# Moving the low half of the next head's rotated query from VectorE to GpSimd in an attention and FFN kernel

## The reference

```python
DIM_Q, H, K, D_C, D_CQ, R = (512, 16, 128, 128, 384, 64)
q_hk = (hidden_q @ Wq.T).reshape(Bv, Sv, H, K)
q_big = jnp.einsum('bshk,hkq->bshq', q_hk, w_kc_q)
q_big = _apply_rope(q_big, sin_q[None, :, None, :], cos_q[None, :, None, :])
kv_r = _apply_rope(kv_c, sin_k[None], cos_k[None])
q_r = jnp.einsum('bshq,hqr->bhsr', q_big, W_qr)
k_r = jnp.einsum('bld,hdr->bhlr', kv_r, W_kr)
scores = jnp.einsum('bhsr,bhlr->bhsl', q_r, k_r)
attn = jax.nn.softmax(scores, axis=-1)
ctx_c = jnp.einsum('bhsl,bld->bhsd', attn, kv_r)
ctx_lat = jnp.einsum('bhsd,hkd->bhsk', ctx_c, w_kc_kv)
ctx = ctx_lat.transpose(0, 2, 1, 3).reshape(Bv, Sv, H * K)
return ctx @ Wo.T
```

## Time and profile before

| | before |
|---|---|
| median of 3 runs | 858.98 us (858.0 to 860.82) |
| span of the profiled execution | 861.5 us |
| PE busy | 757.3 us, 88% |
| DVE busy | 766.2 us, 89% |
| ACT busy | 573.6 us, 67% |
| POOL busy | 577.6 us, 67% |
| mean granted TensorE clock | 0.966 |
| chain that ended last | PE 35%, POOL 20%, DVE 18%, issue 11%, DMA 7%, SPq 5%, ACT 3% |

### The profile page before, as it was taken

One profiled execution on the slowest core, in us unless ns is written; L12 is line 12 of the kernel. 1 busy time (PEld: TensorE's weight loads), 2 busy tenths in 40 slices (PEclk: granted clock), 3 DMA queues, 4 the chain that ended last, 5 costly groups with the idle time before them and its releaser, 6 DMA issues.

```text
span 861.5 us, 12578 instructions
## 1 busy us (share of the span) xinstructions
PE 757.3 (88%) x3268; PEld 487.1 (57%) x3268; DVE 766.2 (89%) x1026; ACT 573.6 (67%) x838; POOL 577.6 (67%) x581
## 2 busy tenths in 40 slices
PE   3678998989999999999999999999999675868996
PEld 3555565756666666666566656665666442424543
DVE  5799899989998999899989999999999767797895
ACT  2477677767766867687667766776777576774332
POOL 5769674867486757766776668576848474867462
PEclk9889999999999999999999999999999797889999
DMA  9216867776768576858676766677668999400000
GB/s 330 79 49 115 169 130 140 138 167 134 151 114 170 117 161 132 170 111 167 118 160 134 152 128 138 149 137 150 125 146 213 241 227 275 164 0 25 13 24 37
DMA packets 294405, 118.50 MB, mean 138 GB/s; under 512 B 271856, under 2 KB 278000, under 8 KB 294128
## 3 DMA queue, kind: packets, MB, share of 16 engines
q1 hardware_dynamic: 293568, 116.68, 62.0%
q10 hardware_dynamic: 816, 1.57, 0.5%
HBM read 49.02 MB, written 2.10 MB: 59 GB/s over the span
## 4 chain that ended last, share of the span: by engine, by line
PE 35%; POOL 20%; DVE 18%; issue 11%; DMA 7%; SPq 5%; ACT 3%; POOLq 1%; DVEq 0%; ACTq 0%
PE banks L1419 22%; POOL rot_cos L1055 5%; PE scores L1720 5%; DMA load<-in_pack 4%; POOL rot_lo L1063 4%; SPq L943 4%; PE scores L1507 3%; PE banks L1735 3%; DVE neg_max L1323 3%; POOL rot_hi L1061 2%; DVE rows L1330 2%; POOL rot_sin L1046 2%; DVE rot_cos L1295 2%; DVE cv_lo L1288 1%; POOL wq_lo L388 1%
## 5 line engine op out<-in xcount | busy, mean ns | idle before, releaser
L1185 ACT ACTIVATE scores<-scores,neg_max 128x1024 f32<-128x1024 f32 x128 | 139.2, 1087 | 56.1 <-DVE neg_max L1323 54.6
L1330 DVE SCALAR_TENSOR_TENSOR rows<-scores,rows 128x1024 f16<-128x1024 f32 x128 | 154.9, 1220 | 13.7 <-ACT rows L1196 12.6
L1419 PE MATMUL banks<-pt,v_hi 128*128 128x512 f16 x512 | 154.3, 383 | 12.5 <-DMA pt<-rows 11.4
L1323 DVE TENSOR_REDUCE neg_max<-scores 128x1 f32<-128x1024 f32 x128 | 155.5, 1216 | 2.9 <-PE scores L1507 2.7
L1055 POOL TENSOR_TENSOR rot_cos<-rot_cos,rot_sin 128x512 f32<-128x512 f32 x93 | 119.2, 1281 | 46.6 <-DVE rot_sin L1297 42.2
L1196 ACT ACTIVATE rows<-scores 128x1024 f16<-128x1024 f32 x128 | 130.8, 1022 | 5.2
L1063 POOL TENSOR_TENSOR rot_lo<-rot_cos,rot_hi 128x512 fp32r<-128x512 f32 x93 | 119.6, 1286 | 7.8
L1159 ACT CAST cv_hi<-banks 128x512 fp32r<-128x512 f32 x64 | 37.6, 587 | 102.6 <-PE banks L1419 101.4
L1318 DVE SCALAR_TENSOR_TENSOR acc<-banks,inv,acc 128x512 f32<-128x512 f32 x128 | 91.4, 745 | 8.0 <-PE banks L1419 4.1
L1419 PE MATMUL banks<-pt,v_lo 128*128 128x512 f16 x256 | 97.8, 382 | 0.0
L1419 PEld LDWEIGHTS banks<-pt,v_hi 128*128 128x128 f16 x512 | 44.5, 98 | 79.2 <-issue 36.4
(11 more groups left out here) (211 smaller groups left out, 1824.7 us busy)
## 6 DMA issues: line engine op xcount, KB each, us to landing
load<-in_pack SPq DMA_DIRECT2D x15, 320.0 KB, 3.5
raw_chunk<-in_out_w SPq DMA_DIRECT2D x8, 512.0 KB, 5.2
raw_chunk<-in_gate_w SPq DMA_DIRECT2D x8, 512.0 KB, 4.4
raw_chunk<-in_val_w SPq DMA_DIRECT2D x8, 512.0 KB, 4.6
raw<-in_gate_w SPq DMA_DIRECT2D x8, 512.0 KB, 5.5
raw<-in_val_w SPq DMA_DIRECT2D x8, 512.0 KB, 5.2
raw<-in_out_w SPq DMA_DIRECT2D x8, 512.0 KB, 7.0
load<-in_pack SPq DMA_DIRECT2D x15, 256.0 KB, 3.3
```

The lines of the kernel that those rows point to most:

```text
L1185: nc.scalar.activation(scores[:, u % 2, :], scores[:, u % 2, :], ACT.Exp, bias=neg_max[:, u:u + 1], accum_out=sums[:, u:u + 1]).then_inc(e ...
L1323: nc.vector.tensor_reduce(neg_max[:, u:u + 1], scores[:, u % 2, :], AX, ALU.max, negate=True).then_inc(max_ready, 1)
L1330: nc.vector.scalar_tensor_tensor(out=rows[:, u % ROWS, 1, :], in0=scores[:, u % 2, :], scalar=WEIGHT_LIFT, in1=rows[:, u % ROWS, 0, :], op ...
L1419: mm = nc.tensor.matmul(out, ws[a], xs[c], start=first and n == 0, stop=last and n == 2)
```

## The change

For the queries of heads 1 to 15 (C0 and C1 with "next"):

- ACT copies the whole bank (128 rows, fp32) to `rest`, and rows 0 to 63 to qr_hi rows 0 to 63. This is all that is read from the bank, and PE's wait for it is on ACT's count `group_hi`.
- POOL, from the entries C0 and C1 of its order, writes `upper_rest` (rest rows 0 to 63 less qr_hi), a tile in the place of qr_hi rows 64 to 127, waits for it, and writes qr_lo rows 64 to 127 (rest rows 64 to 127 plus upper_rest). It counts `query_low` and waits for that itself.
- ACT's doubling waits for `query_low`, and copies both qr_hi and qr_lo, so it is two instructions in place of one.
- DVE's two instructions and the entries C0 and C1 in its orders are gone.

The opening's own query, head 0's, stays as it was. The core of the diff:

```diff
 EVEN_POOL = (
-    ("w", 2), ("rot", 0, 0), ("rot", 0, 1), ("rot", 0, 2), ("w", 3), ("rot", 1, 0), ("rot", 1, 1), ("rot", 1, 2),
-    ("w", 0), ("w", 1),
+    ("w", 2), ("rot", 0, 0), ("rot", 0, 1), ("rot", 0, 2), ("w", 3), ("rot", 1, 0), ("rot", 1, 1), C0, ("rot", 1, 2),
+    ("w", 0), C1, ("w", 1),
 )
...
+    def bank_copied(self, group):
+
+        g, earlier = self.bank_last_used(group)
+        if g is None or not by_pool(g):
+            return None
+        if earlier:
+            return self.start_hi + self.before_highs.index(g) + 1 - len(self.before_highs)
+        return self.hi(g)
...
+        upper_rest = nc.alloc_sbuf_tensor_at("upper_rest", [P, B, S], F32, offset=at["qr_hi"])
...
+            def query_rest(p, marked):
+
+                b, low = marked[1], slice(R, 2 * R)
+                n = p.head.plus(1).after(B, b + 1 - B)
...
+                pool.wait_ge(group_hi, p.hi(marked))
+                if p.head.i is not None:
+                    apart()
+                nc.gpsimd.tensor_tensor(upper_rest[low, b, :], rest[0:R, b, :], qr[0][0:R, b, :].bitcast(F32),
+                                        ALU.subtract).then_inc(query_rested, 1)
+                pool.wait_ge(query_rested, n)
+                if p.head.i is not None:
+                    apart()
+                nc.gpsimd.tensor_tensor(qr[1][low, b, :], rest[low, b, :], upper_rest[low, b, :], ALU.add).then_inc(query_low, 1)
+                pool.wait_ge(query_low, n)
...
+                elif by_pool(marked):
+                    nc.scalar.copy(rest[:, group[1], :], src)
+                    out, src = qr[0][0:R, group[1], :], banks[0:R, p.bank[marked], :]
...
             def double(p, marked):
 
                 b = marked[1]
-                done = p.earlier(("C", b, "next")) if marked[-1] == "last" else p.place(("C", *marked[1:]))
-                act.wait_ge(group_read, p.read(done))
+                if p.first and len(marked) == 2:
+                    act.wait_ge(group_read, p.emptied_at(("C", b)))
+                else:
+                    h = p.head if marked[-1] == "last" else p.head.plus(1)
+                    act.wait_ge(query_low, h.after(B, b + 1 - B))
+                    nc.scalar.copy(qr[0][R:2 * R, b, :], qr[0][0:R, b, :])
                 nc.scalar.copy(qr[1][0:R, b, :], qr[1][R:2 * R, b, :]).then_inc(doubled, 1)
...
+                if not k and p.bank_copied(marked) is not None:
+                    pe.wait_ge(group_hi, p.bank_copied(marked))
```

More of the change, by code:

```diff
@@ L123 @@
     ("O", 1, 2, "last"), ("low", 3), ("O", 1, 3, "last"), A1, ("max", 4), ("M",), ("B", 1, 0, "next"),
-    ("B", 1, 1, "next"), ("max", 5), C0, ("low", 4), ("low", 5), ("K", 0, 0, "next"), ("K", 0, 1, "next"),
+    ("B", 1, 1, "next"), ("max", 5), ("low", 4), ("low", 5), ("K", 0, 0, "next"), ("K", 0, 1, "next"),
     ("B", 1, 2, "next"), V0, ("max", 6), ("O", 0, 0), ("max", 7), ("O", 0, 1), ("low", 6), ("O", 0, 2), ("O", 0, 3),
-    C1,
 )
@@ L271, in sine_by_pool, with by_pool @@
     return group[0] == "B" and group[-1] == "next" and group[1:3] in SIN_BY_POOL
+def by_pool(group):
+    return group[0] == "C" and group[-1] == "next"
 def two_engines(group):
@@ L319, in __init__ @@
             self.before = [(g, BANK[1 - odd][g]) for g in BEGUN[1 - odd]]
-            self.before_full, self.before_emptied = ALL[1 - odd], EMPTIED[1 - odd]
+            self.before_full, self.before_emptied, self.before_highs = ALL[1 - odd], EMPTIED[1 - odd], HIGHS[1 - odd]
             self.start = head.after(GROUPS, GROUPS_BEFORE)
             self.start_hi = head.after(HI_GROUPS, HI_BEFORE)
+            self.start_empty = head.after(EMPTIES, EMPTIES_BEFORE)
     def full(self, group):
@@ L329, in emptied_at @@
     def emptied_at(self, group):
-        return self.start + self.place(group)
+        return self.start_empty + self.place(group)
     def read(self, *places):
-        return self.start + max(places)
+        return self.start_empty + max(places)
     def place(self, group):
@@ L343, in hi, with bank_last_used @@
         return self.start_hi + self.highs.index(group) + 1
-    def bank_free(self, group):
+    def bank_last_used(self, group):
         bank = self.bank[group]
@@ L349, in bank_free @@
             if self.bank[g] == bank:
-                return self.place(g)
+                return g, False
         for g, used in reversed(self.before):
             if used == bank:
-                return self.before_emptied.index(g) + 1 - len(self.before_emptied)
-        return None
+                return g, True
+        return None, False
+    def bank_free(self, group):
+        g, earlier = self.bank_last_used(group)
+        if g is None or by_pool(g):
+            return None
+        return self.earlier(g) if earlier else self.place(g)
+    def bank_copied(self, group):
+        g, earlier = self.bank_last_used(group)
+        if g is None or not by_pool(g):
+            return None
+        if earlier:
+            return self.start_hi + self.before_highs.index(g) + 1 - len(self.before_highs)
+        return self.hi(g)
     def earlier(self, group):
@@ L1106, in period @@
                 for item in POOL_ORDERS[p.head.number % 2]:
-                    if item[0] == "rot":
+                    if by_pool(item):
+                        query_rest(p, item)
+                    elif item[0] == "rot":
                         b = item[1]
```

25 lines of the change are left out of this document (16 added, 9 removed).

## The result

| | before | after |
|---|---|---|
| median | 858.49 us (856.54 to 860.82, 4 runs) | 920.18 us (920.01 to 925.02, 4 runs) |
| span of the profiled execution | 861.5 us | 918.1 us |
| mean granted TensorE clock | 0.966 | 0.939 |
| DVE busy | 766.2 us | 723.7 us |
| POOL busy | 577.6 us | 654.5 us |

The changed kernel takes 1.0707 times as long (95% interval 1.0674 to 1.074): 61.7 us more by the medians. The forecast was 914 us, and its text gives 905 to 922 for its own spread and reaches down to 890 for the rivals.

The account below looks back on a forecast made before the run. At the end of even periods PE waits for POOL, which was taken to have no slack there. 7 x (6.1 + 1.1) + 5 = 55.4 on the profiled 861.5, against the median 914 us; own spread 905 to 922, reaching to 890.

Parts of the forecast that it names:

- ACT's doubling waiting for POOL with V0 queued behind it: End of even periods: doubling moves to 338.15, O products start at 340.8 instead of 335.80, PE idle for 5.0.
- +6.1: Even period: wc is split until 353.1 and PE starts B at 353.2 instead of 347.15.
- half time on POOL: Rival: POOL's instructions on half the partitions take 0.64, odd periods hide all; 884 us, chance 0.07.
- The clock holds: Rival: PE's 5.0 of idleness brings no half rate, B starts at 351.95, +4.8 per even period; 903 us, chance 0.14.
- faster: Rival: DVE is the bound and POOL's extra work is slack, 2.3 off each pair; 843 us, chance 0.04.
- Nothing on this stretch has slack: End of even periods: POOL's rotations, wq's split, wc's load and split, and PE's start behind them leave no spare time.
- rot_lo ends 1.1 later, and PE waits 1.1 longer: Odd periods: POOL's C0 lasts 2.8, of which 1.75 was idle, so PE's existing wait at 382.24 grows by 1.1.
- a second idle stretch: Part of the case slower than all others, beside C1 being late for more; chance 0.05.
- 7.2: Loss per pair of periods: 6.1 in the even kind plus 1.1 in the odd kind, counted seven times.
- The opening: Opening period, ending like an even one: wc is split some 5 later than it was, +5.
- The 2.3: Even periods: loss from 12 matmuls at half rate after PE's 5.0 idle, making C1 full at 347.3 instead of 345.0.
- 350.2: Even periods: time when wc's load, behind tile 6's transposes on SP, would be in.

Follow-up runs that it names:

- e1: Changed kernel with ACT's doubling of C0 moved behind V0 and tile 6's exponential and high part in even and opening periods; 900.83 us, ratio 1.0469.
- e2: Changed kernel with C0's low part placed ahead of rotations (1,0) and (1,1) in POOL's order, ACT's order unchanged; 897.24 us, ratio 1.0421.
- e5: Changed kernel with C0 put back on DVE, so only C1's low part is made by POOL; 858.88 us, ratio 0.998.
- e6: Changed kernel with C1 put back on DVE, so only C0's low part is made by POOL; 927.55 us, ratio 1.0772.
- e7: Changed kernel with both groups' low instructions on DVE from SBUF, none on POOL, ACT's copies and doublings kept; 866.21 us, ratio 1.0074.
- e4: e3 plus 8 thrown-away products on PE ahead of C1's third part in odd periods; 910.53 us, ratio 1.0575.
- e3: Changed kernel with 20 thrown-away products on PE ahead of the first O group in even periods and the opening; 914.98 us, ratio 1.0627.
- e9: e2 with 15 thrown-away products on PE ahead of C1's first part in even periods and the opening; 883.96 us, ratio 1.0266.

## Why the prediction was right, and where it was off

**Right: the place and the chain of waits.** The forecast rested on ACT's doubling waiting for POOL with V0 queued behind it. It said that ACT would double from 338.15 and the O products start at 340.8 after 5.0 of PE's idle time; they stand at 338.33 and 340.83, after 4.97. B in the even period was put at 353.2 and came at 353.28: +6.1, as said. And C1's end: ACT was to begin its copies at 347.3, POOL to end at 351.3; they did at 347.38 and 351.30. e1 and e2 show that the wait is a real cost and not only a visible one (1.8 and 1.5 of the even period), e5 and e6 that C0 alone carries it.

**Right: the time of a POOL instruction on 64 partitions.** 1.28 was assumed and 1.26 to 1.30 measured, so the rival "half time on POOL" (884) falls. "The clock holds" (903) falls by the rows after 365.89, "faster" (843) by ACT's 4.99 of waiting, since it needed POOL to be ready before ACT; and e5 shows, for C1's half, that even where POOL takes the work at no cost the time that DVE saves moves nothing. One sentence went too far: "Nothing on this stretch has slack". POOL's pause before wc's load held C1 (e5) and 0.57 us of longer rotations (e7) without a later B.

**Off: the odd period.** The step "rot_lo ends 1.1 later, and PE waits 1.1 longer" was right for the wait (1.2: C1's third part follows B after 36.30, before after 35.09), but I stopped there. The idle stretch of 2.00 that this makes is followed by the level of 1.2 GHz as well, in six of the seven odd periods, and costs 1.7 (B after 8.94 for 7.20; 1.6 by e4, whose 7.36 leaves 0.16 that is not the clock's). I had asked what the clock does after the gap of 5.0 and not after the one of 2.0, though the earlier trace rows has gaps of 3.05 and 4.30 only and so said nothing of 2.0; "a second idle stretch" stood only in the last case, at 0.05. So a pair is 6.1 + 1.2 + 1.7 = 9.0, not 7.2; the trace has 8.9.

**Off by little.** The opening costs 4.4, not 5. The seventh pair with the last period costs 5.2, less than the others: its odd period has no fall to half rate (idle stretch 1.63), and the head after its even period has no successor, so there is no wc to split at its end. Sum: 4.4 + 6 x 8.9 + 5.2 = 63 up to the first `hidden` of the FFN, which starts at 808.96, before at 745.88. The two spans then differ by only 56.6, since the FFN was 6.5 shorter in this execution. The medians, 61.7 apart, show that little of that is kept in most runs. So it is luck that the profiled span, 918.1, lies only 1.2 above the sum (861.5 + 55.4): the odd periods were priced too low, and the FFN's stretch, which is no part of the argument, gave most of it back.

**Right where it fell, smaller where it counts: the clock in the even period.** The 2.3 was right for the O products and C1: C1's first product starts 5.15 after the first O (371.04 less 365.89), before 2.80. Of that, 1.3 was to reach B; by e3 it is 0.9 at best, because wc's load, which I had put at 350.2, came at 350.7: without the fall B comes at 352.5 and not at 351.95. The prediction had 6.1 with the fall and 4.8 without; it is 6.1 and 5.3.

**What makes a pair's 8.9.** Even kind, 5.9: POOL's delay of the rotations 2.8 (e9), the clock 0.7 (e3), and by difference 2.4 for ACT's wait with V0 behind it. Odd kind, 3.0: the clock 1.6 (e4), POOL's delay 1.2, and 0.2 not taken apart. This is an estimate, since the terms come from different kernels and needn't add. The 2.4 is no measurement of its own: e1 takes the wait away and makes a new idle stretch of 3.81 in its place.

## What to carry to other kernels

Before work goes from a busy engine to an idler one, look at what the receiving engine has in its queue behind the new work and whether others wait for that at that place: the same two instructions were free in POOL's pause before a load (e5) and cost over 60 us where POOL had no pause (e6). And when a moved result feeds a wait, look at what stands behind the waiting instruction: here a copy whose result was needed much later held the one that PE needed at once.

Price every idle stretch of PE that a change makes or lengthens twice, once for itself and once for the matmuls behind it, and then ask whether something else, a load for instance, was to end just as late.

## What the runs showed of the chip

- **Idle stretches and the clock.** PE came back at the lower level after 3.57, 3.81 and 4.97 of idle time every time in the steady state, and never after the 1.47 of e2's odd periods. After about 2.0 in odd periods it was not settled: six of six in the changed kernel (1.99 to 2.02), but four of six in e3 and in e6 and three of six in e1 (1.96 to 2.00). This one of e3 kept full rate (0.24 from the second start to the third):

```profile
230.69 0.50 PE L1523 MATMUL banks<-rot_hi,wr 128*128 128x512 f32 x1 [1.96 <-POOL rot_lo L1086]
231.02 0.40 PE L1523 MATMUL banks<-rot_lo,wr 128*128 128x512 f32 x1
231.26 0.39 PE L1472 MATMUL banks<-kt_hi,wk_hi 128*128 128x512 f32 x1
```

- **POOL on 64 partitions.** A tensor_tensor of 64x512 took 1.26 to 1.30, as one of 128x512 did. The Trainium skill's "GPSIMD Engine Reference", section "2. Architecture", gives each core its own 16 partitions; the trace agrees in that half of the partitions saved nothing.
- **DVE beside POOL.** In e7 a DVE tensor_tensor of 64x512 with both inputs in SBUF took 0.98 (qr_lo) beside POOL's rotations and 0.69 otherwise; with the one ahead of it (0.73) it went along with a rot_hi 0.24 and a rot_lo 0.33 longer. In the kernel before, with one input in PSUM, the same two instructions took 0.69 each beside rotations of 0.62 and 1.27 (rot_hi at 330.06 and rot_lo at 330.77).
